# Two attention visits and a routing regrouped in a macaron block of expert FFNs around linear attention

## The chip, the cores and the metric

The kernel runs on one core of a Trainium2 chip. The metric is device time in microseconds (us) of one execution; the kernel before has a median of 237.55 us over three runs (236.08 to 238.13).

## The reference, cut to what matters

The input x is 2 batches of 2048 tokens of width 128, all f32. A routed FFN, a linear attention and the same routed FFN again are added to it, each behind a layer norm.

```python
x = x + 0.5 * ffn(layernorm(x))
x = x + attn(layernorm(x))
x = x + 0.5 * ffn(layernorm(x))

def ffn(x):    # 4 experts, D 128, hidden 512; each token uses the expert of its largest gate logit
    idx = argmax(softmax(x @ Wg + bg))
    return (gelu(x @ W1[idx] + b1[idx]) @ W2[idx] + b2[idx])

def attn(x):   # P = 32 features
    q, k, v = x @ Wq.T, x @ Wk.T, x @ Wv.T
    qp, kp = elu(q @ proj) + 1, elu(k @ proj) + 1
    kv = kp.T @ v                        # 32 x 128, over all tokens of the batch
    return (qp @ kv) / (sum(qp, -1) + 1e-8)
```

## The kernel before, in words

**Phases and visits.** One FFN over one batch is a phase: 0 and 1 are the first FFN over batches 0 and 1, 2 and 3 the second. Before a phase the batch's 16 tiles of 128 tokens are gathered in the order of their experts, by indirect DMAs that GpSimd issues (`gather`, L418). A tile that straddles two experts is computed once for each, with a mask, so a phase has V = 16 + 3 = 19 visits, and the program 76. I write u9 for visit 9 of the phase spoken of. A visit has four `up` products (L966, PSUM banks U), four GELUs on ScalarE (`gelu`, L1145), four `down` products (L977, banks DN) and one VectorE operation that adds the result into the row tile G (`finish`, L729). TensorE works three visits ahead with `up`: after `down` of u(v) comes `up` of u(v+3). Norms (`norm`, L705) and transposes (`turn_in`, L957; copied by ScalarE's `copy_in`, L1139) of the tiles come some visits ahead by the tables NORM_LATE, NORM_MID (phase 1), NORM_EARLY (phase 2) and GROUP_AT. `down` of u(v) waits for `finish` of u(v-2).

**Attention** of batch 0 runs inside phase 1, that of batch 1 inside phase 2, beside the FFN of the other batch. It goes by four groups of four tiles: transposes into bank S1 (`side_turn`, L991), a copy by ScalarE (`side_copy`, L1154), the key, query and gate products (`side_kq`, L998), scaled by VectorE (`la_scaled`, L750 to L752), exp on ScalarE (`la_exp`, L1176), elu and the scaled keys (`la_features`, L758 and L762), the sum over tokens (`la_sum`, L1009), the division (`la_z`, L770 to L773), a fold and the product with Wv (`la_fold`, `la_kv`), the transposed queries (`la_q`, L1021). Then for each group `lb_num` (L1033) makes the result in S1, and `lb_x2` (L793 to L799) adds it to x and takes mean and variance; the next group's `lb_num` waits until the add L793 has read S1. GpSimd raises the variance to -1/2 (`pow_lb`, L406).

**Routing of the second FFN** follows in the same phase, by the number HOT1: `route_hot` at u(HOT1) on VectorE marks each token's expert (hot); `counts` on TensorE counts them; `route_slots` on VectorE (L637 to L651) makes each token's place and the one-hot table A; `place_lanes` and `hots` on ScalarE, `place_tiles` on GpSimd (AV from A) and `route_hots` on VectorE (L656, SL) make the operands of `inverse` (L940, 16 small bf16 products), whose result `route_src` turns into the row indices that `gather` of the next-but-one phase reads. `visit_tables` and `visit_masks` follow later.

**The order** of the work is written out by hand, one list for each engine, indexed by phase and visit; semaphores connect them. GpSimd's list is one queue: the powers, `place_tiles`, and all 64 gathers and 32 scatters. A scatter (`scatter`, L442) writes one finished tile of the second FFN to the output. Ahead of most DMAs stands a memset of a spare tile (L416; 512 or 256 columns), which waits until the previous DMA is issued. In phase 2 GpSimd issues 7 scatters of batch 0 between its other work, then from u(FIRST1) = u11 the 16 gathers of phase 3, and then, outside the visit loop, the 25 remaining scatters.

Of the kernel before, what the change touches and what calls it, by code (L numbers as in the profile page):

```python
# [34 lines left out]
def build(nc, x, wq, wk, wv, proj, w1, b1, w2, b2, wg, bg, out):  # L35
# [31 lines left out]
    with ExitStack() as ctx:  # L67
# [142 lines left out]
        NORM_MID = (-5, -4, -3, -2, -1, 0, 0, 1, 1, 2, 2, 3, 4, 5, 7, 8)  # L210
        NORM_EARLY = (-5, -4, -3, -2, -1, 0, 0, 1, 1, 2, 2, 3, 4, 5, 6, 6)
# [59 lines left out]
        HOT0, HOT1 = 5, 7  # L271
# [89 lines left out]
        def _(eng):  # L361
# [117 lines left out]
            SCATTERS = {5: (1,), 6: (2,), 7: (3,), 8: (4,), 9: (5,), 10: (6,)}  # L479
            DONE0, PAIRS1 = 7, 10  # L480
# [51 lines left out]
        def _(eng):  # L532
# [299 lines left out]
            for s in range(2 * B * V):  # L832
                ph, v = divmod(s, V)
                f, b = divmod(ph, 2)
                finish(s)
# [425 lines left out]
```

How the kernel before makes its waits and increments, by code:

```python
def need(eng, stage, j):  # L17
    if j >= 0:
        eng.wait_ge(stage.sem, j + 1)
# [8 lines left out]
    def did(self, instruction, wait=True):  # L28
        instruction.then_inc(self.sem, 1)
        self.n += 1
        if wait:
            self.eng.wait_ge(self.sem, self.n)
# [257 lines left out]
        @block.sync  # L290
# [12 lines left out]
            def store_x(b, h):  # L303
                for i in range(h * XN[b] // 2, (h + 1) * XN[b] // 2):
                    eng.wait_ge(s_x[b][i], 16)
                eng.dma_start(rows0_v[b][:, h * H:(h + 1) * H, 0:D], X0[b][:, h * H:(h + 1) * H, :]).then_inc(s_rows0[b], 16)
# [22 lines left out]
                ph, v = divmod(s, V)  # L329
                if v % CHUNK == (s == 1):
                    need(eng, rt["visit"], ph)
                    v -= v % CHUNK
                    offs.update({ph * V + v + i: e for i, e in enumerate(loaded(eng, v_slab, ph, v, SW))})
                k = s % NSLAB
                need(eng, ffn["hT"], s - NSLAB)
                need_res(eng, s - NSLAB)
                eng.dma_start(slab[k][:, :], W1[:, bass.ds(offs[s], SW)]).then_inc(s_slab[k], 16)
            eng.wait_ge(s_w["w1"], 16)
            eng.wait_ge(s_w["b2"], 16)
            eng.wait_ge(s_foldd, 4)
# [17 lines left out]
        @block.gpsimd  # L360
# [8 lines left out]
            for b in range(B):  # L369
                eng.memset(MR0[b][:, :, :], 0.0).then_inc(s_const, 1)
            eng.wait_ge(s_const, 7)
            for b in range(B):
# [158 lines left out]
        @block.vector  # L531
# [2 lines left out]
            did = chain.did  # L534
            eng.wait_ge(s_const, 17)
            eng.memset(ones_b[:, :], 1.0).then_inc(s_constd, 1)
```

## Time and profile before

| what | us |
|---|---|
| median of the runs shown | 237.55 |
| the profiled execution's own time | 237.53 |
| its span, first to last instruction | 235.8 |
| TensorE busy | 207.2 (88%) |
| GpSimd busy | 160.2 (68%) |
| VectorE busy | 159.4 (68%) |
| ScalarE busy | 126.9 (54%) |

In the profile PE is TensorE's product and PEld its weight load, DVE is VectorE, ACT ScalarE, POOL GpSimd. "Idle before" is how long an engine stood still ahead of an instruction, with what ended the wait; "issue" means that nothing which the profile shows was waited for. The profiled execution is 1.7 us longer than its span, for what lies around the program. The profile names scatters out_dram<-G L442 and gathers G<-rows,src L430.

### The profile page before, as it was taken

The page shows a single profiled execution, that of the slowest core. Times are in us where ns is not written, and L with a number is a line of the kernel's source. Part 1 is how long each engine was busy: PE and PEld are TensorE (multiplying, and loading weights), DVE is VectorE, ACT ScalarE, POOL GpSimd, SP SyncE. Part 2 cuts the span into 40 slices and gives each one's busy share as a digit, 9 for nine tenths or more (in the row PEclk, how much of TensorE's full clock was granted, in tenths as well). Part 3 has the DMA queues.
Part 4 walks back from the last instruction along what each step waited for, and adds up shares of the span by engine and source line. Part 5 has one row for each costly group of instructions (what it writes and reads, how often), then busy time and mean ns, then how long its engine had stood idle before and what let it go on. Part 6 is the DMA issues. An engine that isn't in the chain of part 4 may idle for free. (4 is left out here: it accounts for less than half of the span.)

```text
span 235.8 us, 6375 instructions
## 1 busy us (share of the span) xinstructions
PE 207.2 (88%) x1786; PEld 195.7 (83%) x1786; DVE 159.4 (68%) x641; ACT 126.9 (54%) x406; POOL 160.2 (68%) x225
## 2 busy tenths in 40 slices
PE   8989996996997999999969998999959899999900
PEld 7879996896997988889969897779959899999900
DVE  3699463579688989698887879788776545553400
ACT  1415055567554586635675676825565567765500
POOL 7221888882728687147138888756878888788775
PEclk9999999998899999999999999999979999999985
DMA  4999259982534462326703852517721976662111
GB/s 103 372 321 254 96 199 351 314 212 83 185 110 167 154 215 69 130 106 237 277 0 116 300 206 83 165 61 281 269 79 42 329 274 222 222 221 103 45 56 45
DMA packets 28454, 41.69 MB, mean 177 GB/s; under 512 B 7795, under 2 KB 14851, under 8 KB 28422
## 3 DMA queue, kind: packets, MB, share of 16 engines
q1 hardware_dynamic: 22368, 34.11, 40.5%
q0 software_dynamic: 3072, 6.82, 11.1%
q10 hardware_dynamic: 2982, 0.36, 1.0%
q8 instruction: 16, 0.26, 0.5%
q14 instruction: 16, 0.13, 0.2%
HBM read 9.41 MB, written 6.82 MB: 69 GB/s over the span
## 5 line engine op out<-in xcount | busy, mean ns | idle before, releaser
L1145 ACT ACTIVATE hT<-U,slab 128x128 f32<-128x128 f32 x304 | 86.7, 370 | 56.4 <-PE U L966 56.3
L966 PE MATMUL U<-hT_in,slab 128*128 (+1 forms) x608 | 82.8, 280 | 1.5 <-ACT hT_in L1139 1.3
L977 PE MATMUL DN<-W,hT 128*128 (+1 forms) x608 | 83.7, 282 | 0.2 <-issue 0.2
L966 PEld LDWEIGHTS U<-hT_in,slab 128*128 128x128 f32 x608 | 74.8, 194 | 2.7 <-issue 2.4
L977 PEld LDWEIGHTS DN<-W,hT 128*128 128x128 f32 x608 | 75.4, 195 | 1.4 <-issue 1.2
L430 POOL DMA_INDIRECT G<-rows,src x64 | 62.5, 977 | 15.2 <-issue 10.2
L729 DVE SCALAR_TENSOR_TENSOR G<-DN,mask,G 128x128 f32 (+1 forms) x76 | 26.4, 348 | 27.3 <-PE DN L977 24.6
L416 POOL MEMSET rest<- 128x512 f32 (+1 forms) x78 | 35.4, 454 | 6.3 <-DVE G L729 0.7
L442 POOL DMA_INDIRECT out_dram<-G x32 | 31.6, 988 | 7.3 <-issue 6.3
L705 DVE TENSOR_SCALAR xn<-G 128x128 f32<-128x128 f32 x64 | 23.7, 389 | 9.3 <-DMA G<-rows,src 9.0
L717 DVE SCALAR_TENSOR_TENSOR G<-slab,mask,G 128x128 f32 (+1 forms) x60 | 21.2, 353 | 6.7 <-DVE G L729 4.0
L1139 ACT ACTIVATE hT_in<-TR 128x128 f32<-128x128 f32 (+1 forms) x44 | 14.4, 327 | 17.8 <-PE TR L957 17.4
L957 PE MATMUL TR<-ident,xn 128*128 128x128 f32 x64 | 14.6, 280 | 7.5 <-DVE xn L705 6.3
L401 POOL TENSOR_TENSOR RS<-VE,neghalf 128x4 f32<-128x4 f32 x8 | 8.5, 1062 | 12.9 <-DVE VE L741 12.8
L406 POOL TENSOR_TENSOR G<-VE,neghalf 128x4 f32<-128x4 f32 x8 | 8.3, 1043 | 12.8 <-DVE VE L799 12.6
L957 PEld LDWEIGHTS TR<-ident,xn 128*128 128x128 f32 x64 | 8.3, 142 | 8.8 <-DVE xn L705 7.2
L898 PE MATMUL DN<-mean_w 128*128 128x128 f32 x104 | 14.6, 300 | 1.1 <-POOL mean_w L362 1.1
L898 PEld LDWEIGHTS DN<-mean_w 128*128 128x128 f32 x104 | 13.9, 215 | 1.1 <-POOL mean_w L362 1.1
L467 POOL TENSOR_TENSOR AV<-A,lane_f 128x256 bf16<-128x256 bf16 x4 | 3.3, 828 | 12.5 <-DVE A L651 6.9
L396 POOL TENSOR_TENSOR MR<-VE,neghalf 128x8 f32<-128x8 f32 x4 | 6.7, 1679 | 5.7 <-DVE VE L564 5.2
L734 DVE BATCH_NORM_STATS2 ST<-G 128x6 f32<-128x128 f32 x32 | 8.8, 287 | 1.6 <-issue 1.4
L656 DVE TENSOR_TENSOR SL<-slot_i,lane_b 128x512 bf16<-128x512 int32 x12 | 8.8, 784 | 0.0
(159 smaller groups left out, 219.7 us busy)
## 6 DMA issues: line engine op xcount, KB each, us to landing
slab<-W SPq DMA_DIRECT2D x76, 322.0 KB, 3.1
rows<-G SPq DMA_DIRECT2D x8, 288.0 KB, 2.1
rows<-X SPq DMA_DIRECT2D x4, 512.0 KB, 9.5
X<-in_L_attn_x_dram SPq DMA_DIRECT2D x4, 256.0 KB, 6.7
X<-in_L_attn_x_dram SPq DMA_DIRECT2D x2, 512.0 KB, 8.8
W<-in_L_ffn_W_dram SPq DMA_DIRECT2D x1, 1024.0 KB, 11.5
W<-in_L_ffn_W_dram SPq DMA_DIRECT2D x4, 256.0 KB, 6.0
G<-rows,src POOLq DMA_INDIRECT x64, 3.2
```

The source lines that it names most:

```text
L416: eng.memset(rest[:, 0:columns], 0.0)
L430: eng.indirect_dma_start(out=row(f, b, t, 0, RW), out_offset=None, in_=(rows0, rows1)[f][b], in_offset=bass.IndirectOffsetOnAxis(ap=src[f] ...
L442: eng.indirect_dma_start(out=out_rows, out_offset=bass.IndirectOffsetOnAxis(ap=index, axis=0), in_=row(1, b, t), in_offset=None, engine_se ...
L705: ffn["norm"].done(eng.tensor_scalar(xn[k % NXN][:, :], row(f, b, t), row(f, b, t, D, 1), row(f, b, t, D + 1, 1), ALU.subtract, ALU.mult))
L717: ffn["res"].done(eng.scalar_tensor_tensor(out=r, in0=slab[s % NSLAB][:, F + NC:SW], scalar=mask[f][b][:, v:v + 1], in1=r, op0=ALU.mult, o ...
L729: ffn["out"].done(eng.scalar_tensor_tensor(out=r, in0=DN[s % 2][:, 0:D], scalar=mask[f][b][:, v:v + 1], in1=r, op0=ALU.mult, op1=ALU.add))
L898: eng.matmul(DN[0][:, 0:P], mean_w[:, :], mean_w[:, :], start=True, stop=True)
L957: last = eng.transpose(TR[:, i * P:(i + 1) * P], xn[k % NXN][:, :], ident[:, :])
L966: i = eng.matmul(U[s % 3][:, c * P:(c + 1) * P], slab[s % NSLAB][:, c * P:(c + 1) * P], hT_in[ph % 2][:, bass.ds(v * P - expert_at[s], P)] ...
L977: i = eng.matmul(DN[s % 2][:, 0:D], hT[s % NHT][:, c * P:(c + 1) * P], W2[:, bass.ds(expert_at[s] + c * NE * D, D)], start=(c == 0 and not ...
L1139: ffn["xTs"].done(eng.activation(hT_in[ph % 2][:, first * P:(first + n) * P], TR[:, 0:n * P], ACT.Copy))
L1145: i = eng.activation(hT[s % NHT][:, c * P:(c + 1) * P], U[s % 3][:, c * P:(c + 1) * P], ACT.Gelu, bias=slab[s % NSLAB][:, F + c:F + c + 1])
```

## The change

- TensorE: `side_turn` of group 3 comes ahead of `down` of u0 and `side_kq` at u0 (was u1). `la_fold` moves from u3 to u2, `la_kv` and `la_q` stand together in u3. The four `lb_num` are at u3, u4, u4, u5 (were u4, u4, u5, u6).
- ScalarE: one run of four exps at u0 behind the copy of group 3 (was three at u18 of the phase before and one at u1), so no copy or wait lies between them; the table loads stay two in each of these phases.
- VectorE: `la_scaled` of group 3 at u0 behind the norms; features in two runs of two groups; one `la_z` over all 16 tiles (was 12 and 4); `lb_x2` at u3, u4, u5, u5 (were u4, u4, u5, u6). The norm tables of phases 1 and 2 leave u1 and u2 free and put two norms each into u3, u4 and u5.
- Routing: HOT1 is 6 instead of 7. `counts` comes at u8, ahead of `up`, instead of u9 behind it; `inverse` at u10 in both phases (was u11 in phase 1, u10 in phase 2). In `route_slots` two small operations (end_i, flo_i) leave for `visit_tables`.
- GpSimd: FIRST1 becomes 10, so phase 3's gathers begin in u10; 6 scatters stand ahead of them instead of 7, and 26 behind them instead of 25.

```diff
-        NORM_MID = (-5, -4, -3, -2, -1, 0, 0, 1, 1, 2, 2, 3, 4, 5, 7, 8)
-        NORM_EARLY = (-5, -4, -3, -2, -1, 0, 0, 1, 1, 2, 2, 3, 4, 5, 6, 6)
+        NORM_MID = (-5, -4, -3, -2, -1, 0, 0, 0, 3, 3, 4, 4, 5, 5, 7, 8)
+        NORM_EARLY = (-5, -4, -3, -2, -1, 0, 0, 0, 3, 3, 4, 4, 5, 5, 6, 6)
...
-        HOT0, HOT1 = 5, 7
+        HOT0, HOT1 = 5, 6
...
-                if ph > 0 and v == 4:
-                    pow_lb(o, 0)
-                if ph == 2 and v == 4:
-                    scatter(0, 0)
-                if ph > 0 and 4 <= v < 3 + NG:
-                    pow_lb(o, v - 3)
+                if ph > 0 and v in (4, 5, 6):
+                    pow_lb(o, v - 4)
+                if ph > 0 and v == 6:
+                    pow_lb(o, 3)
...
-            SCATTERS = {5: (1,), 6: (2,), 7: (3,), 8: (4,), 9: (5,), 10: (6,)}
-            DONE0, PAIRS1 = 7, 10
+            SCATTERS = {v: (v - 4,) for v in range(4, FIRST1)}
+            DONE0, PAIRS1 = FIRST1 - 4, 10
...
-                if v >= FIRST1:
+                if FIRST1 <= v < FIRST1 + T // 2:
...
-                did(eng.tensor_copy(end_i[:, :], c3[:, 0:NE - 1, T - 1]))
-                did(eng.tensor_scalar(flo_i[:, :], end_i[:, :], 7, None, ALU.arith_shift_right))
...
-                    if v == 4:
-                        lb_x2(o, 0)
                         lb_x2(o, 1)
-                    if v in (5, 6):
-                        lb_x2(o, v - 3)
+                    if v == 5:
+                        lb_x2(o, 2)
+                        lb_x2(o, 3)
...
+                if ph in (1, 2) and v == 0:
+                    side_turn(o, NG - 1)
                 down(s)
+                if ph in (1, 2):
+                    if v == 3:
+                        la_kv(o)
+                        la_q(o)
+                    if v == 4:
+                        lb_num(o, 1)
+                    if v == 5:
+                        lb_num(o, 3)
...
-                if ph == 0 and v == hot_at + 2:
+                if ph < B + 1 and v == hot_at + 2:
                     counts(ph + 1)
...
-                    if v == hot_at + 2:
-                        counts(ph + 1)
-                    if v == hot_at + (3 if ph == 2 else 4):
+                        la_fold(o)
+                    if v in (3, 4):
+                        lb_num(o, 2 * (v - 3))
+                    if v == hot_at + 4:
                         inverse(ph + 1, 0, NG)
...
-                if late and v == 1:
-                    la_exp(ph - 1, 3, 4)
...
                         side_copy(o * NG + NG - 1)
+                        la_exp(o, 0, NG)
...
-                if ph < B and v == 18:
-                    la_exp(ph, 0, 3)
```

The first place is TensorE in phase 2, where the counts of the routing stand. U are `up` products, DN `down` products, TR transposes, and S<-hot the counts. Before, end of `down` of u9 and what follows:

```order
L977 ISA
L977 MATMUL DN<-W,hT 128x128
L966 ISA
L966 MATMUL U<-hT_in,slab 128x128 x4
L930 MATMUL S<-hot,ones_b 128x64
L931 MATMUL S<-hot,below_b 128x64
L974 ISA
L974 MATMUL DN<-B2s,ones_b 128x128
```

Now, end of `down` of u8 and what follows:

```order
L977 ISA
L977 MATMUL DN<-W,hT 128x128
L957 MATMUL TR<-ident,xn 128x128 x2
L930 MATMUL S<-hot,ones_b 128x64
L931 MATMUL S<-hot,below_b 128x64
L966 ISA
L966 MATMUL U<-hT_in,slab 128x128 x4
L264 TENSOR_LOAD v_exp_0
```

The counts moved ahead by two `up` and one `down`; `inverse` of this phase stands where it stood.

The second place is VectorE in phase 1, from the writing of KV on: G_1<-DN is a `finish`, G_0<-S with the three rows behind it one `lb_x2`, xn a norm. Before:

```order
L786 TENSOR_TENSOR KV<-S,blocks 128x512
L705 TENSOR_SCALAR xn<-G_1 128x128
L729 ISA
L729 SCALAR_TENSOR_TENSOR G_1<-DN,mask_1,G_1 128x128
L793 TENSOR_TENSOR G_0<-S,G_0 128x4x128
L796 BN_STATS ST_0<-G_0 128x6 x4
L798 BN_AGGR G_0<-ST_0 128x2 x4
L799 TENSOR_SCALAR VE_0<-G_0 128x4
```

Now:

```order
L785 TENSOR_TENSOR KV<-S,blocks 128x512
L728 SCALAR_TENSOR_TENSOR G_1<-DN,mask_1,G_1 128x128
L704 TENSOR_SCALAR xn<-G_1 128x128 x2
L792 TENSOR_TENSOR G_0<-S,G_0 128x4x128
L795 BN_STATS ST_0<-G_0 128x6 x4
L797 BN_AGGR G_0<-ST_0 128x2 x4
L798 TENSOR_SCALAR VE_0<-G_0 128x4
L728 ISA
```

The first `lb_x2` now stands behind the `finish` of u3 and two norms, a `finish` of u4 behind it; before, the first two `lb_x2` stood together behind the `finish` of u4.

The third place is GpSimd behind the loop, where the scatters change from batch 0 (G_0) to batch 1 (G_1). Before:

```order
L416 MEMSET rest 128x256
L442 DMA out_dram<-G_0 4096x128 x2
L416 MEMSET rest 128x256
L442 DMA out_dram<-G_0 4096x128
L442 DMA out_dram<-G_1 4096x128
```

Now:

```order
L416 MEMSET rest 128x256
L442 DMA out_dram<-G_0 4096x128 x2
L416 MEMSET rest 128x256
L442 DMA out_dram<-G_1 4096x128 x2
L416 MEMSET rest 128x256
```

One more scatter of batch 0 stands here, and the last run of scatters with no memset between them is behind the eleventh memset instead of the tenth.

## Rows read from the trace of the kernel before

**Rows 1.** The page: busy time of each engine, and the granted clock in 40 slices.

```profile
PE 207.2 (88%) x1786; PEld 195.7 (83%) x1786; DVE 159.4 (68%) x641; ACT 126.9 (54%) x406; POOL 160.2 (68%) x225
...
PEclk9999999998899999999999999999979999999985
```

**Rows 2.** Groups of POOL's instructions from 176 to 236 us: count, busy, mean, idle before.

```profile
L442 POOL DMA_INDIRECT out_dram<-G x25 | 24.2, 967 | 6.2 <-issue 5.3 <-DVE G L729 0.9
L430 POOL DMA_INDIRECT G<-rows,src x16 | 15.4, 965 | 2.7 <-issue 2.7
L416 POOL MEMSET rest<- 128x256 f32 x26 | 8.1, 312 | 1.6
```

**Rows 3.** Timeline of POOL: start, us, instruction, idle before it and its releaser.

```profile
171.56 0.61 POOL L467 TENSOR_TENSOR AV<-A,lane_f 128x256 bf16<-128x256 bf16 x1 [0.60 <-DVE A L651]
...
176.05 0.31 POOL L416 MEMSET rest<- 128x256 f32 x1
...
233.20 0.95 POOL L442 DMA_INDIRECT out_dram<-G  x1 [0.30 <-issue]
```

**Rows 4.** Timeline of PE in phase 2: down of u7, counts, inverse.

```profile
162.46 1.11 PE L977 MATMUL DN<-W,hT 128*128 x8
...
168.31 0.19 PE L930 MATMUL S<-hot,ones_b 128*128 128x64 bf16 x1
...
172.87 0.25 PE L940 MATMUL S<-AV,SL 128*128 128x32 bf16 x4 [2.22 <-DVE SL L656]
...
173.98 0.40 PE L940 MATMUL S<-AV,SL 128*128 128x32 bf16 x8 [0.34 <-DVE SL L656]
```

**Rows 5.** The chain that ended last: start, us, what.

```profile
174.49 1.90 PE DN L977 x8
176.39 1.23 PE U L966 x8
...
223.57 0.36 DVE G L729
```

**Rows 6.** Timeline of DVE: the slots of the routing in phase 1, then in phase 2.

```profile
114.53 0.29 DVE L637 TENSOR_TENSOR_SCAN cum<-S,zeros 128x64 f32<-128x64 f32 x1 [0.48 <-PE S L931]
...
115.25 0.16 DVE L643 CAST end_i<-cum 128x3 int32<-128x3 f32 x1
...
116.40 0.42 DVE L651 TENSOR_TENSOR A<-tile_i,lane_f 128x256 bf16<-128x256 int32 x1
...
117.00 2.31 DVE L656 TENSOR_TENSOR SL<-slot_i,lane_b 128x512 bf16<-128x512 int32 x3
...
168.56 0.29 DVE L637 TENSOR_TENSOR_SCAN cum<-S,zeros 128x64 f32<-128x64 f32 x1 [0.45 <-PE S L931]
...
169.29 0.57 DVE L643 CAST end_i<-cum 128x3 int32<-128x3 f32 x1
...
171.06 0.42 DVE L651 TENSOR_TENSOR A<-tile_i,lane_f 128x256 bf16<-128x256 int32 x1
```

**Rows 7.** Timeline of PE in phase 1: down of u0, a turned tile, down of u7.

```profile
84.49 1.06 PE L977 MATMUL DN<-W,hT 128*128 x8
...
88.48 0.30 PE L957 MATMUL TR<-ident,xn 128*128 128x128 f32 x1 [0.60 <-ACT hT_in L1139]
...
107.99 1.11 PE L977 MATMUL DN<-W,hT 128*128 x8
```

**Rows 8.** Waits of PE from 80 to 190 us: total, times, longest.

```profile
PE U L966 <- ACT hT_in L1139: 1.3, 1, 1.3
PE S L991 <- DVE KM L752: 1.2, 2, 0.7
```

**Rows 9.** Timeline of ACT in phase 1: three exps, then the copy of group 3.

```profile
87.15 1.03 ACT L1176 ACTIVATE KM<-KM 128x256 f32<-128x256 f32 x3
...
88.24 0.58 ACT L1154 ACTIVATE xTs<-S 128x512 f32<-128x512 f32 x1
```

**Rows 10.** Timeline of DVE in phase 1: the first addition of `lb_x2`.

```profile
99.73 0.69 DVE L793 TENSOR_TENSOR G<-S,G 128x512 f32<-128x512 f32 x1 [0.71 <-PE S L1034]
```

More of the change, by code:

```diff
@@ L641, in route_slots @@
                 need(eng, rt["cb"], ph)
-                did(eng.tensor_tensor(wh3[:, :, :], wh[:, :, :], hot[:, :, :], ALU.mult), False)
-                did(eng.tensor_copy(end_i[:, :], c3[:, 0:NE - 1, T - 1]))
-                did(eng.tensor_reduce(pos[:, :], te(wh3), AX.X, ALU.add), False)
-                did(eng.tensor_scalar(flo_i[:, :], end_i[:, :], 7, None, ALU.arith_shift_right))
+                did(eng.tensor_tensor(wh3[:, :, :], wh[:, :, :], hot[:, :, :], ALU.mult))
+                did(eng.tensor_reduce(pos[:, :], te(wh3), AX.X, ALU.add))
                 did(eng.tensor_copy(pos_i[:, :], pos[:, :]))
@@ L661, in visit_tables @@
                 e_no = exp_no[:, 1:NE, 0]
+                ends = cum[:, :].rearrange("p (e t) -> p e t", e=NE)[:, 0:NE - 1, T - 1]
+                did(eng.tensor_copy(end_i[:, :], ends))
+                did(eng.tensor_scalar(flo_i[:, :], end_i[:, :], 7, None, ALU.arith_shift_right))
                 did(eng.scalar_tensor_tensor(out=vis[:, :], in0=flo_i[:, :], scalar=float(T - 1), in1=e_no, op0=ALU.min,
@@ L880, in _ @@
                     if v == 0:
-                        la_features(o, 0, NG - 1)
-                    if v == 1:
-                        la_z(o, 0, NG - 1)
+                        la_features(o, 0, 2)
+                    if v == 3:
+                        lb_x2(o, 0)
                 if ph < B + 1:
@@ L1018, in la_q @@
             def la_q(b):
-                need(eng, la["z"], 2 * b + 1)
+                need(eng, la["z"], b)
                 for g in range(NG):
@@ L1074, in _ @@
                 ph, v = divmod(s, V)
+                hot_at = HOT0 if ph == 0 else HOT1
+                o = ph - 1
+                if ph in (1, 2) and v == 0:
+                    side_turn(o, NG - 1)
                 down(s)
+                if ph in (1, 2):
+                    if v == 3:
+                        la_kv(o)
+                        la_q(o)
[3 more added lines that the diff above has]
+                        lb_num(o, 3)
                 for ahead in groups_of(ph, v):
                     turn_in(*ahead)
-                hot_at = HOT0 if ph == 0 else HOT1
                 if ph in (1, 2):
-                    o = ph - 1
                     if v == 0:
-                        side_turn(o, NG - 1)
-                    if v == 1:
                         side_kq(o, NG - 1)
-                    if v == 3:
-                        la_q(o)
-                        la_fold(o)
-                    if v in (4, 5, 6):
-                        lb_num(o, (0, 2, 3)[v - 4])
-                if ph == 0 and v == hot_at + 2:
+                    if v == 2:
+                        la_sum(o, 2, 4)
+                if ph < B + 1 and v == hot_at + 2:
                     counts(ph + 1)
@@ L1209, in _ @@
                 late = ph in (1, 2) and v in (0, 1, 2)
-                if late and v == 1:
-                    la_exp(ph - 1, 3, 4)
-                if late and v > 0:
-                    gelu(s + UP_LEAD - 1)
                 if ph in (1, 2):
@@ L1217, in _ @@
                         side_copy(o * NG + NG - 1)
+                        la_exp(o, 0, NG)
                     if v == 2:
                         la_part(o)
+                if late and v > 0:
+                    gelu(s + UP_LEAD - 1)
+                if ph in (1, 2):
                     if v == 3:
```

15 lines of the change are left out of this document (5 added, 10 removed).

## The prediction, made before the changed kernel ran

> **What bounds the kernel now.** I read the page first. TensorE is busy 88% of the span, GpSimd 68% [rows 1], so TensorE looks like the bound. Then I asked which engine is never idle at the end. The groups of GpSimd from 176 us on hold 25 scatters, 16 gathers and 26 memsets, with 24.2 + 15.4 + 8.1 = 47.7 us busy and 10.5 us idle. Nearly all of that idle time is "issue", 0.15 to 0.3 us ahead of each DMA [rows 2]. Three scatters name a `finish` of VectorE, 0.9 us in all, but their gaps are no longer than the others, so they did not really wait. The last scatter starts at 233.20, while the last `finish` started at 223.57 [rows 3, 5]. So the end is set by a queue: GpSimd works without a pause from 176.05 to 234.15, 58.1 us, and TensorE's end has some 9 us of slack behind which it may hide. The chain of waits on the page passes from GpSimd to TensorE at 224, which is only the releaser it inferred for a wait of zero length.
>
> What starts that queue? Ahead of it stands AV at 171.56, behind an idle time of 0.60 that ended with A of VectorE; then two scatters (171.56 to 176.05 is 4.49 us) and the first gather's memset [rows 3]. The row indices for that gather come from `inverse`, which ended near 174.4, so at 176.05 they had been there for over a microsecond: GpSimd itself was late. Thus the quantity that decides is the moment A is ready in phase 2, 171.06 + 0.42 = 171.48 [rows 6]. The end is 64.3 us after it.
>
> I count from T7, the start of `down` of u7 in phase 2, 162.46 [rows 4]. A is ready at T7 + 9.0.
>
> **The routing, from T7 to A.** Between T7 and the counts lie today three `down` (0.95 each), three `up` (0.89) and a pair of transposes (0.22): 5.85 us, 162.46 to 168.31 [rows 4]. The change takes away a `down` and two `up`, so TensorE reaches the counts at T7 + 3.1. VectorE must have written hot by then. It works on `lb_x2` of group 3 in u5 now, a visit earlier; its step from there to hot is some 3 us, and I get T7 + 2.9 for it, a tie with TensorE. The first operation of the slots, cum, starts 0.25 after the counts: T7 + 3.3. From cum to A ready took 116.82 - 114.53 = 2.29 us in phase 1 and 171.48 - 168.56 = 2.92 us in phase 2 [rows 6]. Two operations go out of it, about 0.15 us net, since each was issued beside another. That leaves 2.1 to 2.8; I take 2.5. So A is ready at T7 + 5.8 instead of + 9.0: 3.2 us.
>
> The two moved operations cost some 0.4 us in `visit_tables` at u11, behind everything named here.
>
> Why the two phases differ bears on this term. The conversion into end_i took 0.16 us in phase 1 and 0.57 in phase 2 [rows 6]; in phase 1 GpSimd stood still then, in phase 2 it was issuing scatters. The Trainium skill, GPSIMD Engine Reference, Specifications, says that GpSimd shares its SBUF interfaces with VectorE, so that the two contend in some VectorE operations. By that rule the chain is 2.1 wherever GpSimd rests and 2.8 where it works, and A would shift by no more than 0.4 either way of my value. The rows show the difference, not its cause.
>
> **TensorE's stall at `inverse`.** It waited 2.2 us for SL and, with the two pieces behind it, about 2.8 [rows 4], and then ran at a lower clock: `down` took 1.90 and `up` 1.23 where 0.95 and 0.89 are usual, 1.3 us more [rows 5], in the slice in which the page's granted clock falls to 7 tenths [rows 1]. With the counts 1.5 visits earlier, SL is ready at T7 + 5.8 + 0.3 (a `finish`) + 2.3 (three operations, [rows 6]) = T7 + 8.4, and TensorE comes to `inverse` at T7 + 3.1 + 4.8 = 7.9, so a stall of some 0.6 to 1 us stays and the clock should hold. TensorE is thus 3.2 us or more better off here. By the queue above that is worth nothing in itself; only A counts.
>
> **The price in GpSimd's queue.** Two scatters stand between AV and the first gather, as before. But one more scatter stands behind the gathers, with one more memset. A scatter with its gap takes (24.2 + 6.2) / 25 = 1.22 us, a memset with its gap (8.1 + 1.6) / 26 = 0.37 [rows 2]. So the queue from A on grows by 1.6 us, from 64.3 to 65.9. The removed scatter saves nothing, because it stood ahead of A, where GpSimd now will wait longer for A.
>
> **How T7 moves.** Three pieces.
> First, attention, from `down` of u0 to `down` of u7 in phase 1: 84.49 to 107.99, 23.5 us [rows 7]. Adding up the products alone gives about 21.4, so about 2.1 us are waits, the largest known one 0.60 for the copy of a turned tile behind the exps [rows 7]. Those go, since the copy now follows the GELU. New waits come. TensorE asks for the key and query products only 0.1 us after it has turned the next tile, and must wait for that tile's copy and the copy of group 3 (0.58, [rows 9]): 1.0 us. The product of group 3 stands right behind `down` of u5, but needs the addition of group 2, which VectorE does after the `finish` of u5: 0.35 and 0.69 [rows 10] and two signals, 1.25 us. One more wait of 0.2 is at group 2. The sum is 2.5 for 2.1: I forecast 0.3 us slower, and nothing gained by moving. The four exps end at about 89.5 in the time of before (a first exp 0.42 us, then 0.3 each: [rows 9] has 1.03 for three), and the GELU of u3 follows 3 us later, about 1.2 ahead of its `down`. The `la_z` of all groups ends a visit before `la_q` asks for it. So neither is the last wait.
> Second, `inverse` in phase 1. The wait of 1.3 us for ScalarE's copy [rows 8] goes, because ScalarE's part now comes a visit earlier. Another comes: the norm of tile 15 stands in u8 of VectorE behind the three SL operations (2.31, [rows 6]), and the transposes of u10 ask for it 1.3 us too early. One wait takes the other's place; with the shorter way I put the balance at 0.5 us gained.
> Third, side transposes waited for KM 1.2 us in two places in phase 1 [rows 8]; with the tables a visit earlier VectorE is less behind: 0.4 gained.
> Phase 1 gives 0.6 us in all; phase 2's attention I set equal. T7 comes to 161.9.
>
> **Sum.** A at 161.9 + 5.8 = 167.7, 3.8 us earlier; the queue behind it 1.6 longer; span 235.8 - 3.8 + 1.6 = 233.6, and the execution's own time 237.53 - 2.2 = 235.3. The median of the runs shown, 237.55, is the same number. A measurement tells about 1% from no change here, 2.4 us, so the forecast stands just at that line.
>
> Bounds: the slot chain 2.1 to 2.9 (0.4 either way); T7 from 5 us earlier (all new waits of both phases absent) to 1 us later (the phase 1 balance lost as well); AV 0.6 us as in rows 3, or up to a half more. Together 230 to 237; the ends need everything at once.
>
> **Rivals.**
> - *TensorE sets the end.* The Trainium skill, Perfetto Trace Analysis, Identifying the Most-Contended Engine, has one take the engine of highest occupancy as the bound, here TensorE. As a mechanism: the scatters behind the gathers would wait for `finish`, and the end would follow TensorE's stalls. TensorE gains 2.8 + 1.3 - 0.7 at `inverse` and about 0.8 from phase 1: 4.2, so 233.3. For it speaks the page's 88%; against it the slack of 9 us at the end [rows 3, 5].
> - *The new attention waits are half as long.* 1.25 us less in each phase, T7 earlier by 2.5: 232.8. For it: VectorE and ScalarE are idle a third and a half of the time. Against it: the wait for the addition of group 2 is fixed by the written order.
> - *The gain is eaten.* The slots take 2.9, AV half a microsecond more, T7 does not come earlier: A at 162.8 + 3.3 + 2.9 and AV + 0.5, 2.0 us gained, 1.6 given to the extra scatter: 237.1.
> - *Slower: attention starves TensorE in u4 and u5.* `lb_x2` of groups 1 to 3 with two `finish`, four norms and the statistics fill VectorE without a hole; if it falls a microsecond behind, the product of group 3 waits 2.5 instead of 1.25, and the clock falls as it did behind the 2.2 us wait (1.3 us). That is 2.6 per phase, 5.2 in both: 240.5. It costs more than the gain as soon as the two phases together lose 2.2 us. Against it: in u4 and u5 I find VectorE ready half a microsecond ahead of TensorE.
>
> **How the numbers follow.** Forecast 45%, half of it under 235.2; TensorE as the bound 10%; shorter waits 15%; gain eaten 20%; starved 10%. Faster by over 1%: 0.22 + 0.10 + 0.15 and a little, 0.48. Within 1%: 0.23 + 0.19, 0.42. Slower 0.10. The range runs from the case of shorter waits to the eaten gain, 232.7 to 237.4, which leaves the starved case and a tenth of the rest outside.
>
> **What would show it.** In the changed profile GpSimd should stand idle 1 to 2 us ahead of AV in phase 2, then work without a pause to the end, 65.9 us after A; 26 scatters behind the gathers; `inverse` in phase 2 waiting about 1 us for SL, with no slow product behind it; a wait of about 1.2 us of the product of group 3 (L1033) in u5 of both phases; transposes of phase 1 waiting for the norm of tile 15. The argument is wrong if GpSimd pauses among its last scatters, if the end moves by other than A's shift less 1.6, or if T7 moves by more than 2 us.

## The result, and the profile after

The changed kernel takes 243.41 us (median of 4 runs, 242.84 to 244.72), the kernel before 236.81 beside it (4 runs, 235.76 to 238.13): ratio 1.028, 95% interval 1.021 to 1.036. It is slower by 6.6 us; the forecast was 2.2 us faster, and the time lies outside its range of 232.7 to 237.4. The experiments ran on several chips. On two of them every kernel, before included, takes 11 to 19 us more, nearly all of it in the last phase, so times are compared by ratio to the kernel before that ran beside them, and across chips by distances in the trace. On the others before takes 236.39 to 237.28.

The page of the changed kernel, busy time and granted clock:

```profile
PE 207.3 (86%) x1786; PEld 194.0 (80%) x1786; DVE 157.8 (65%) x633; ACT 127.6 (53%) x406; POOL 160.3 (66%) x225
...
PEclk9999999999999999999999999799999999999955
```

All engines have their work of before to within 2 us ([rows 1]), in a span 6.4 us longer (242.2 against 235.8). The loss is waiting.

First the end, where the forecast looked. Groups of POOL from 181.5 to 242 us, the answer to [rows 2]:

```profile
L442 POOL DMA_INDIRECT out_dram<-G x26 | 25.1, 965 | 6.3 <-issue 5.1 <-DVE G L728 1.2
L430 POOL DMA_INDIRECT G<-rows,src x16 | 15.5, 968 | 2.7 <-issue 2.7
L416 POOL MEMSET rest<- 128x256 f32 x26 | 8.2, 314 | 1.6
```

POOL's timeline, as [rows 3]:

```profile
176.42 0.62 POOL L465 TENSOR_TENSOR AV<-A,lane_f 128x256 bf16<-128x256 bf16 x1 [1.88 <-DVE A L647]
...
239.60 0.96 POOL L442 DMA_INDIRECT out_dram<-G  x1 [0.31 <-issue]
```

GpSimd waits 1.88 us for A, then works without a pause to 240.56. From AV to there it is 64.1 us, against 234.15 - 171.56 = 62.6 before: 1.5 more for the extra scatter, as forecast (1.6). PE and DVE in phase 2, as [rows 4] and [rows 6]; one fence for each engine:

```profile
170.67 1.11 PE L977 MATMUL DN<-W,hT 128*128 x8
...
173.94 0.20 PE L930 MATMUL S<-hot,ones_b 128*128 128x64 bf16 x1
...
179.33 0.56 PE L940 MATMUL S<-AV,SL 128*128 128x32 bf16 x16
```

```profile
174.21 0.29 DVE L635 TENSOR_TENSOR_SCAN cum<-S,zeros 128x64 f32<-128x64 f32 x1
...
175.91 0.42 DVE L647 TENSOR_TENSOR A<-tile_i,lane_f 128x256 bf16<-128x256 int32 x1
```

As in the prediction, T7 is the start of `down` of u7 in phase 2, here 170.67, and A is the moment at which the one-hot table A is ready. The counts stand at T7 + 3.3, the slots take 175.91 + 0.42 - 174.21 = 2.1 us, A is ready at 176.33, T7 + 5.7. `inverse` waits for nothing and the clock holds. So the part that the change was about works as worked out. But T7 is 170.67 where [rows 4] has 162.46.

Where does T7 come from? Waits of all engines, 80 to 190 us: total, times, longest (compare [rows 8]):

```profile
DVE LGX L749 <- POOL RS L401: 6.4, 2, 3.9
...
PE S L1033 <- DVE G L792: 3.0, 4, 1.3
...
PE S L1009 <- DVE KR L761: 2.3, 1, 2.3
...
PE TR L957 <- DVE xn L704: 2.2, 3, 1.0
...
PE S L998 <- ACT xTs L1155: 1.7, 2, 0.9
```

The largest, 6.4 us, names an operation that the prediction never speaks of: VectorE waits for RS, the power (variance to -1/2) that GpSimd computes for the attention groups (`pow_la`, L401). `la_scaled` (L749 to L751) cannot begin without it. Now both sides of that wait. POOL's timeline at the turn from phase 1 to phase 2:

```profile
137.23 1.04 POOL L401 TENSOR_TENSOR RS<-VE,neghalf 128x4 f32<-128x4 f32 x1
...
140.75 0.96 POOL L430 DMA_INDIRECT G<-rows,src  x1 [0.16 <-issue]
...
142.51 0.96 POOL L430 DMA_INDIRECT G<-rows,src  x1 [0.15 <-issue]
...
144.27 0.96 POOL L430 DMA_INDIRECT G<-rows,src  x1 [0.15 <-issue]
...
146.03 0.96 POOL L430 DMA_INDIRECT G<-rows,src  x1 [0.15 <-issue]
147.02 1.04 POOL L401 TENSOR_TENSOR RS<-VE,neghalf 128x4 f32<-128x4 f32 x1
```

DVE there:

```profile
138.38 0.17 DVE L749 COPY LGX<-S 128x16 f32<-128x16 f32 x1 [2.47 <-POOL RS L401]
...
141.95 0.43 DVE L740 TENSOR_SCALAR VE<-MV 128x4 f32<-128x4 f32 x1
...
148.16 0.17 DVE L749 COPY LGX<-S 128x16 f32<-128x16 f32 x1 [3.90 <-POOL RS L401]
```

And PE, which pays:

```profile
140.03 0.33 PE L957 MATMUL TR<-ident,xn 128*128 128x128 f32 x1 [0.96 <-DVE xn L704]
...
150.16 0.99 PE L1009 MATMUL S<-G,KR 128*32 128x128 f32 x16 [2.28 <-DVE KR L761]
...
153.70 1.97 PE L966 MATMUL U<-hT_in,slab 128*128 x8
```

The variance of group 3 is written at 142.4, but its power runs at 147.02: the gathers of GpSimd stand ahead of it in the queue, one every 1.76 us. FIRST1 = 10 starts those of phase 1 a visit earlier too, so 12 gathers instead of 10 lie ahead of that power, and the change asks for `la_scaled` of group 3 a visit sooner (u0 instead of u1). Behind the wait, the sum over tokens waits 2.28 us, and an `up` then takes 1.97 us instead of 1.06, at a granted clock of 0.57 between 152 and 156 us, the 7 in the page's row.

Against [rows 4, 7], counted by the starts of `down`, the loss grows so: 84.51 to 109.02 is 24.5 us for u0 to u7 of phase 1 where before has 23.5 (+1.0); at the first `down` of phase 2 it is +3.4 (141.91 against 138.49); at its u7 +8.2. So the stretch of attention in phase 1 costs 1.0, the rear of phase 1 2.4, the first seven visits of phase 2 4.8. The counting moves a little from one stretch to the next: the four transposes of group 3 (some 0.4 us) now stand ahead of the first `down` of a phase, so they fall to the rear of phase 1 and no longer to the visits behind it.

### The profile page after: what moved, and what is told of

Same layout as the page of the kernel before. It is cut to its first block, busy times and chain, and to the rows that moved or that the text cites. A ratio compares the mean times of both kernels' runs of the same rounds, so it can differ in the third digit from the quotient of the medians.

```text
span 242.2 us, 6366 instructions
## 1 busy us (share of the span) xinstructions
PE 207.3 (86%) x1786; PEld 194.0 (80%) x1786; DVE 157.8 (65%) x633; ACT 127.6 (53%) x406; POOL 160.3 (66%) x225
## 4 chain that ended last, share of the span: by engine, by line
PE 36%; DVE 13%; POOL 8%; issue 6%; DMA 4%; DVEq 1%; ACT 0%; POOLq 0%
PE DN L977 15%; PE U L966 14%; DMA G<-rows,src 3%; POOL out_dram L442 3%; POOL rest L416 3%; DVE G L792 2%; DVE ST L795 2%; PE TR L957 2%; DVE G L728 2%; PE S L1033 2%; POOL G L430 2%; POOL RS L401 1%; PE S L998 1%; PE S L1009 1%; DVE G L797 1%
## 5 line engine op out<-in xcount | busy, mean ns | idle before, releaser
L977 PE MATMUL DN<-W,hT 128*128 (+1 forms) x608 | 81.8, 278 | 1.2 <-DVE G L728 0.8
L977 PEld LDWEIGHTS DN<-W,hT 128*128 128x128 f32 x608 | 73.8, 192 | 2.3 <-issue 2.2
L957 PE MATMUL TR<-ident,xn 128*128 128x128 f32 x64 | 15.2, 289 | 7.5 <-DVE xn L704 7.4
L401 POOL TENSOR_TENSOR RS<-VE,neghalf 128x4 f32<-128x4 f32 x8 | 8.3, 1042 | 11.2 <-DVE VE L740 11.1
L1033 PE MATMUL S<-KV,QT 128*128 128x512 f32 x16 | 8.8, 630 | 3.0 <-DVE G L792 3.0
L998 PE MATMUL S<-Wkq,xTs 128*128 128x96 f32 x64 | 8.5, 275 | 1.7 <-ACT xTs L1155 1.7
```

The costliest lines, as they stand in the source:

```text
L957: last = eng.transpose(TR[:, i * P:(i + 1) * P], xn[k % NXN][:, :], ident[:, :])
L977: i = eng.matmul(DN[s % 2][:, 0:D], hT[s % NHT][:, c * P:(c + 1) * P], W2[:, bass.ds(expert_at[s] + c * NE * D, D)], start=(c == 0 and not ...
```

## The experiments

Theory Q: the powers stand behind more gathers in GpSimd's one queue. Its rival S: the written order of the attention visits is what costs. For a single wait of TensorE in u5 there are W (the wait itself costs time) and V (VectorE is full, and TensorE's waits only mirror it). For the end there are G (the queue from A on sets it) and E (TensorE or `finish` sets it). All kernels below differ from the changed kernel or from before only in what is said of them.

To compare across chips I use two distances in the trace. They came out alike to within 0.1 us wherever the same code ran in that stretch (Z on the chips with the usual last phase only): from the first `finish` of phase 1 to A of phase 2 ready (P), and from AV to GpSimd's last instruction (Z). P + Z moves with the end as long as GpSimd sets it.

| kernel | us | ratio to before, 95% | P | Z |
|---|---|---|---|---|
| before | 236.81 | 1 | 85.9 | 62.6 |
| changed | 243.41 | 1.028 (1.021 to 1.036) | 90.7 | 64.1 |
| e1 gathers of phase 1 from u11 | 238.13 | 1.005 (1.002 to 1.007) | 85.9 | 64.1 |
| e2 routing part alone | 243.08 | 1.023 (1.016 to 1.029) | 90.2 | 64.9 |
| e3 attention part alone | 240.22 | 1.012 (1.005 to 1.019) | 88.2 | 62.8 |
| e4 e2 with gathers from u11 | 240.54 | 1.013 (1.006 to 1.019) | 87.5 | 64.2 |
| e6 e1, product of group 3 behind `up` | 254.23 | 1.018 (1.011 to 1.026) | 85.9 | - |
| e7 e6, norm 15 before the one-hots | 253.35 | - | 86.0 | - |
| e8 changed, shorter memsets in phase 1's gathers | 257.36 | 1.030 (1.023 to 1.037) | 90.3 | - |
| e9 changed, one power earlier | 250.50 | 1.015 (1.005 to 1.026) | 86.5 | - |
| e13 the same kernel, another chip | 238.83 | 1.010 (1.006 to 1.014) | 86.4 | 64.1 |
| e10 e9, a second power earlier | 250.15 | 1.014 (1.001 to 1.027) | 86.9 | - |
| e5, e12 before, shorter memsets | 252.45, 251.16 | 1.011 (1.003 to 1.018), 1.016 (1.004 to 1.027) | 85.9, 85.9 | - |
| e11 e10, shorter memsets | 253.84 | 1.028 (1.016 to 1.040) | 86.9 | - |
| e14 e13, seven scatters ahead | 237.19 | 1.003 (1.000 to 1.007) | 86.4 | 62.6 |
| e15 e14, gathers from u11 | 236.23 | 0.999 (0.996 to 1.002) | 85.1 | 62.6 |
| e16 before, longer memsets | 241.86 | 1.023 (1.014 to 1.032) | 85.9 | 67.9 |
| e18 before, shorter memsets | 233.84 | 0.988 (0.983 to 0.993) | 85.9 | 60.0 |
| e17 e15, shorter memsets | 233.38 | 0.986 (0.980 to 0.991) | 85.0 | 59.9 |

Before was 237.28 beside e1 to e4, 250.32 beside e5 to e8, 247.91 beside e9 to e12, 236.39 beside e13 to e16, 236.63 beside e17 and e18. So e5 to e8 ran on one of the two chips with the longer last phase and e9 to e12 on the other, and their us figures do not compare with the rest. A dash under Z: there Z says nothing, since GpSimd waits for `finish`. e7 has no ratio, because its four times lie too far apart (249.17 to 254.72).

**Which part costs (e1 to e4).** e1:

```diff
+        G1ST = 11
-                if v >= FIRST1:
-                    gather_first(1, 0, s, v - FIRST1)
+                if v >= G1ST:
+                    gather_first(1, 0, s, v - G1ST)
```

(and the same name where phase 1's gathers are counted). e2 is before with HOT1 = 6, the new places of `counts`, `inverse` and end_i and the new scatters, without the attention part; e3 is the changed kernel with those taken back; e4 is e2 with G1ST = 11.

> The changed kernel with one thing put back: phase 2's rows are gathered from u11 of phase 1 again (10 gathers ahead of the last power instead of 12); counts, inverse and attention stay as changed. Theory Q (the powers of the next batch's attention stand behind more gathers in GpSimd's one queue, and VectorE waits for them): the waits of la_scaled for the power, 2.5 and 3.9 us, shrink to under 1.5 each, and with the later start of attention in phase 2 some 4 to 5 us come back: 238 to 239.5. Rival S (the written order of attention and its own waits, 1.3 us at the product of group 3 and 0.9 at the keys, in both phases): the queue hardly matters and the time stays at 242 or above.

> The kernel before with the routing part of the change alone (counts, inverse, slots, first gathers and the scatters as changed; attention and norm tables as before). Theory Q: A of phase 2 stands 5.7 us behind T7 instead of 9.0, the queue behind it is 1.6 us longer, but the power of group 3 comes some 3 to 5 us late and attention of phase 2 waits for it: 237 to 240. Rival S: the loss comes with attention, so this is faster than before, 234.5 to 235.5.

> The changed kernel with the routing part taken back (HOT1 7, counts, inverse, slots, scatters and gathers as before), so attention and norm tables alone. Theory Q: phase 1 loses 1.0 us up to u7 as in the changed kernel's trace and phase 2 about the same plus up to 1 for the power that is now asked for a visit earlier: 2 to 3 us slower than before, 239 to 240. Rival S: the whole loss is here, 242 or above.

> As e2, but with phase 2's rows gathered from u11 of phase 1. Theory Q: the gain of A without the late powers: 236.8 - 3.2 + 1.6 = 235.2, between 234.3 and 236. Rival S: no better than e2.

e1 gives back 5.3 of 6.6 us with one number (P: 4.8), inside what Q expected. DVE in e1 at the place of the 3.90:

```profile
140.63 0.17 DVE L741 TENSOR_SCALAR VE<-MV 128x4 f32<-128x4 f32 x1
...
144.24 0.17 DVE L750 COPY LGX<-S 128x16 f32<-128x16 f32 x1 [1.49 <-POOL RS L402]
```

e3 is 2.9 us above before, within the 2 to 3 expected. Its waits, with those of e2, show how the two moves meet. In before VectorE waits 0.6 us for the power of group 2 and not at all for that of group 3. It waits 2.4 and 1.4 in e2 (12 gathers, asked for in u1), 0.6 and 1.9 in e3 (10 gathers, asked for in u0), and 2.47 and 3.90 in the changed kernel, which does both.

e2 and e4 came out above their ranges, by 3.1 and 4.5 us. The routing alone, even with the gathers back, is slower than before, and the waits of PE in e4 from 150 to 175 us (total, times, longest) say why:

```profile
PE S L932 <- DVE hot L633: 2.1, 1, 2.1
```

In phase 1 of e4 the same wait is 2.23 more. With the routing a visit sooner but the last attention product and its statistics still at u6, VectorE has both in hand and the counts wait for hot; in phases 1 and 2 of the changed kernel no such wait is over 0.3 us. The two halves of the change need each other, which their separate runs could not show as a sum.

**Is VectorE full, and is it the memset? (e6 to e8).** e6 is e1 with the product of group 3 in u5 moved behind `up`, which should cover most of the 1.3 us wait for the addition; e7 also norms tile 15 before the one-hots; e8 shortens the spare memset ahead of phase 1's gathers from 512 to 128 columns:

```diff
-                gather(f, b, 3 * k // 2)
+                gather(f, b, 3 * k // 2, columns=P)
```

> As e1 (changed kernel, gathers of phase 1 from u11), and the product of group 3 in u5 stands behind up of u8 instead of ahead of it. The wait of 1.3 us for the addition of group 2 is then covered by 0.9 us of up. Theory W (this wait is the written order's and TensorE's time counts up to A of phase 2): 0.9 us less per phase, T7 of phase 2 1.8 us earlier, so 236.3 against 238.1 in e1. Rival V (VectorE is what is full in u4 to u7, and TensorE's waits only mirror it): T7 moves, hot does not, the total stays within 0.5 of e1.

> As e6, and in u8 of phase 1 the norm of tile 15 stands ahead of the one-hots of the routing. The wait of the transposes in u10 of phase 1 (0.8 us) goes: 0.5 to 0.8 us below e6 if TensorE's time counts there; no change if VectorE or GpSimd set the pace of phase 1's end.

> The changed kernel as it is (12 gathers ahead of the last power of phase 1, 26 scatters behind the loop), but with memsets of 128 columns instead of 512 ahead of the gathers that phase 1 issues. Each gather takes some 0.3 us less in GpSimd's queue, so the last power comes about 3.5 us earlier. Theory Q: the waits of 2.5 and 3.9 us for the powers fall below 1 and the total falls to 238.5 to 240 without moving a gather. Rival: if it was not the time in the queue but the gathers' transfers or VectorE's own order that made attention late, it stays above 242.

P is 85.9 and 86.0 against 85.9 of e1: nothing gained, the answer of V. (Their times, on a chip with the longer last phase, can't be set against e1's 238.13.) The waits of PE, 80 to 175 us, in e1:

```profile
PE S L1034 <- DVE G L793: 3.0, 4, 1.3
PE TR L958 <- DVE xn L705: 1.4, 2, 0.8
```

and in e7:

```profile
PE S L933 <- DVE hot L631: 1.7, 2, 1.0
PE S L1036 <- DVE G L793: 1.2, 4, 0.4
```

The wait for the addition falls from 3.0 to 1.2 us and that for the norm goes, and a wait for hot of 1.7 us takes their place. In both, `down` of u7 in phase 1 comes 1.0 us sooner than in e1, as soon as in before, and `down` of u12 no sooner than in e1. VectorE's row of results from u3 to u8 is nearly full (in e1 it is busy 9.4 of the 10 us from 100 to 110), and TensorE meets it at one place or another. e8 missed its forecast. The memset takes 0.20 instead of 0.53 us, but GpSimd's queue hardly moves; two gathers of e8:

```profile
139.58 0.20 POOL L416 MEMSET rest<- 128x128 f32 x1
140.24 0.96 POOL L430 DMA_INDIRECT G<-rows,src  x1 [0.46 <-issue]
141.32 0.20 POOL L416 MEMSET rest<- 128x128 f32 x1
141.98 0.96 POOL L430 DMA_INDIRECT G<-rows,src  x1 [0.46 <-issue]
```

One every 1.74 us, against 1.76 in the changed kernel: the idle "issue" ahead of the DMA grew from 0.16 to 0.46. What holds it there I did not find; in phase 3 the same edit does shorten the step (below). So in this stretch only the place of the power in the queue can help.

**The place of the power (e9, e10, e13).** e9 and e13 are one kernel, the changed one with

```diff
-                if ph < B and v == V - 1:
+                if ph == 0 and v == V - 1:
                     pow_la(ph, NG - 1)
...
+                if v == V - 2:
+                    pow_la(1, NG - 1)
                 if v >= FIRST1:
                     gather_first(1, 0, s, v - FIRST1)
```

so that the power of group 3 stands ahead of the last two gathers of u17. e10 also puts that of group 2 between the two gathers of u13.

> The changed kernel, with one line moved: GpSimd raises the variance of attention group 3 of batch 1 ahead of the last two gathers of u17 instead of behind them. The gathers start in u10 as in the change. Theory Q (the power stands behind too many gathers in GpSimd's one queue, and that is why u7 of phase 2 starts late): the statistics were ready near 142.1, so the power starts near 142.5 instead of 147.02, VectorE's wait of 3.9 us for it in phase 2 shrinks to under 1 us, A of phase 2 comes 4 us earlier and the time is 238.5 to 240, about 1.6% under the changed kernel. Rival S (the written order of the attention visits is what costs): the power comes earlier, but A of phase 2 stays within 1 us of 176.3 and the time at 243.

> As the run before, and the power of group 2 between the two gathers of u13 instead of behind those of u13 and u14. Theory Q: it starts near 134.5 instead of 137.23, the wait of 2.5 us of VectorE in u16 goes, and the rear of phase 1 is up to 1.5 us shorter: 237 to 238.5, at or below the version with gathers from u11 (which measured 238.13 against 237.28). Rival: VectorE is what is full there, and the time is within 0.5 us of the run before.

> The changed kernel with the power of attention group 3 of batch 1 ahead of the last two gathers of u17, again, on whatever chip comes. Theory Q: A of phase 2 is 86.5 us after the first finish of phase 1 (90.7 in the changed kernel, 85.9 in before), and where before has 237 the time is 238.5 to 240. Rival S: the time stays at 243 there.

POOL in e13:

```profile
143.45 1.04 POOL L401 TENSOR_TENSOR RS<-VE,neghalf 128x4 f32<-128x4 f32 x1
```

DVE in e13:

```profile
145.06 0.17 DVE L751 COPY LGX<-S 128x16 f32<-128x16 f32 x1 [0.67 <-PE S L1000]
```

The power starts 3.6 us earlier, VectorE's wait for it is gone (what is left, 0.67, is for the key and query product), and P falls from 90.7 to 86.4, the same on two chips; e13 takes 238.83, ratio 1.010. One power, with all gathers where the change put them, gives back 4.3 us of P and 1.8% of the time (ratio 1.010 for 1.028, intervals that do not meet). That is Q. e10 missed: phase 1 ends 1.6 us sooner, but between the two powers GpSimd issues an unbroken row of five gathers, so that the power of group 3 does not come 1.6 us sooner with it, and VectorE waits 1.8 us for it again: P is 0.4 longer than in e9.

**What sets the end (e16, then e14, e15).** e16 is before with `columns=4 * P` for `columns=2 * P` ahead of phase 3's gathers and of the scatters behind the loop: work that nobody reads, put on GpSimd only.

> The kernel before, with memsets of 512 instead of 256 columns ahead of the gathers of phase 3 and of the scatters behind the loop: 0.21 us more each (0.52 for 0.31), 26 of them in one unbroken queue, 5.5 us. Theory G: the time grows by 4.5 to 5.5 us where before has 237 (242), and all of it lies between AV and the end. Rival E (TensorE sets the end): TensorE has some 9 us of slack behind which the queue would hide, so the time grows by under 1 us. Where before has 248 to 250: if its longer last phase comes from gathers issued too closely, the slower pace gives some of it back.

Its groups of POOL, 176 to 242 us:

```profile
L416 POOL MEMSET rest<- 128x512 f32 x25 | 13.1, 526 | 1.5
```

25 memsets of 256 columns took 7.9 us in e14, so these are 5.2 us longer; P stays 85.9, Z grows by 5.3 and the time by 5.5. TensorE's slack of 9 us hides none of it: G, not E. e14 is e13 with one scatter more ahead of A, where GpSimd stood idle 1.90 us; e15 is e14 with the gathers of phase 1 from u11, as in e1:

```diff
-            SCATTERS = {v: (v - 4,) for v in range(4, FIRST1)}
-            DONE0, PAIRS1 = FIRST1 - 4, 10
+            SCATTERS = {4: (0,), 5: (1,), 6: (2,), 7: (3, 4), 8: (5,), 9: (6,)}
+            DONE0, PAIRS1 = 7, 10
```

> As the run before, and seven scatters instead of six ahead of the gathers of phase 3 (two of them in u7, where GpSimd stood idle 1.88 us ahead of AV), 25 behind. Theory G (the queue from A on sets the end): A does not move, the stretch from AV to GpSimd's end falls from 64.1 to 62.6 and the time by 1.6 us: 237 to 238.4 where before has 237. Rival E: the time stays within 0.5 us of the run before, or A moves later by the scatter's 1.2 us.

> As the run before, and the gathers of phase 1 from u11 as in the kernel before. The version with gathers from u11 measured 238.13 against 237.28 and had waits of 1.49 and 0.59 us of VectorE for the powers; the power of group 3 can now start 1.5 us earlier, and the queue is 1.6 us shorter. Theory Q with G: 235 to 236.3 where before has 237.3, the best version. Rival: VectorE is full, the power's 1.5 us are lost again, 236.5 to 237.

POOL in e15, ahead of AV:

```profile
169.16 0.96 POOL L443 DMA_INDIRECT out_dram<-G  x1 [0.16 <-issue]
170.30 0.62 POOL L466 TENSOR_TENSOR AV<-A,lane_f 128x256 bf16<-128x256 bf16 x1 [0.17 <-DVE A L650]
```

DVE in e15, first and last of the slots:

```profile
168.09 0.29 DVE L638 TENSOR_TENSOR_SCAN cum<-S,zeros 128x64 f32<-128x64 f32 x1
...
169.80 0.42 DVE L650 TENSOR_TENSOR A<-tile_i,lane_f 128x256 bf16<-128x256 int32 x1
```

The scatter fits the hole: AV starts 0.08 after A as before, and from e13 to e14 the idle time falls from 1.90 to 0.18, Z from 64.1 to 62.6, the time by 1.64 us (238.83 to 237.19). e15 takes another 1.3 us off P and reaches before, no more: 0.999, a tie. Its 236.23 lies in the range of 235 to 236.3, but that range was written for a before of 237.3, and the gain of 1 to 2.3 us over before that it implied did not come (0.2); the rival, a full VectorE, is nearer.

**A version that beats both (e5, e11, e12, e17, e18).** If GpSimd's queue sets the end, its memsets are the cheapest thing to shorten: `columns=P` there. e5, e12 and e18 are before with that alone, e17 is e15 with it, e11 is e10 with it.

> The kernel before with nothing but shorter memsets ahead of phase 3's gathers and the scatters behind the loop: 128 columns instead of 256, 26 of them. Theory G (GpSimd's queue sets the end from A on): a memset of 512 columns takes 0.52 us and one of 256 takes 0.31, so one of 128 some 0.2; 26 times 0.1 is 2.7 us off the time from AV to the end (62.6 us), and all of it off the total: 234 to 235. Rival E (TensorE, with the highest occupancy, sets the end): no change, 237.

> As the run before, with memsets of 128 instead of 256 columns ahead of the gathers of phase 3 and of the scatters behind the loop. A memset took 0.20 instead of 0.31 us on the other chip and a gather with its memset 1.37 instead of 1.47. Theory G (GpSimd's queue from A on sets the end): 26 memsets are 0.11 shorter, the stretch from AV to the end shrinks from 64.1 to about 61.5, and the time by 2.5 us to 235 to 236. Rival E (TensorE or the landing of gathers sets it): within 0.7 us of the run before, and GpSimd's last scatters wait for finish.

> The kernel before, with memsets of 128 instead of 256 columns ahead of the gathers of phase 3 and of the scatters behind the loop, as in the run on the other chip, whose last phase was some 13 us longer for every kernel and so could not tell. Theory G: AV to the end of GpSimd shrinks from 62.6 to about 60, time 234.5 to 235.3 where before has 237.3. Rival E: within 0.7 us of before. It counts only if before itself is near 237 in this batch.

> The version that measured 236.23 where before has 236.39 (the change with gathers of phase 1 from u11, the power of group 3 ahead of the last gather of u17, seven scatters ahead of the gathers), with memsets of 128 instead of 256 columns ahead of the gathers of phase 3 and the scatters behind the loop: 25 memsets of 0.20 instead of 0.31 us. Theory G: AV to the end 62.6 - 2.7 = 59.9, time 233 to 234 where before has 236.4, 1.1% faster than before. Rival E: the last scatters wait for finish and the time stays within 0.7 us of 236.2. Where before itself is at 248 to 250 it is slower than before, as the two earlier runs were.

> The kernel before with the shorter memsets alone. Theory G: AV to the end 62.6 - 2.7 = 59.9 and the time 233.7 to 234.5 where before has 236.4. Rival E: within 0.7 us of before. Third possibility: the pace of the gathers itself delays other transfers, TensorE stands still in phase 3 and the time is longer than before on this chip too.

e17 takes 233.38 where before has 236.63, ratio 0.986, and e18 233.84, ratio 0.988. Groups of POOL in e17 from 176 us:

```profile
L417 POOL MEMSET rest<- 128x128 f32 x25 | 5.2, 206 | 1.5
```

7.9 - 5.2 = 2.7 us, and the time fell by 2.85 from e15 to e17. Almost all of it is the memset, which the change had not touched; e17 and e18 do not differ by more than their intervals, so nothing here shows that the regrouped order is worth anything beside the memsets. On the two other chips the same edit made before slower: 252.45 against 250.32 (e5) and 251.16 against 247.91 (e12), where 234 to 235.3 was expected, and e11 takes 253.84 where e10 takes 250.15. I would not recommend it without knowing which chip it meets.

## Why the prediction was wrong

**What failed** is one term, T7, forecast 161.9, measured 170.67: 8.8 us. By the prediction's own sign (T7 moves by more than 2 us) its argument is wrong there. Its pieces, by the words of the prediction:

- "phase 2's attention I set equal". It costs 4.8 us. This is the step that turned the sign. I followed the change to FIRST1 only in phase 3, and the sooner `la_scaled` only on VectorE and TensorE, and never asked what stands behind the moved gathers on GpSimd. Both moves meet in the power of group 3. The move of that power alone returns 4.3 of the 4.8 (e13: `down` of u0 to `down` of u7 takes 24.5 us, 28.8 in the changed kernel, 24.0 in before). It was to be read in the trace of before: POOL ran gathers one every 1.8 us there, and the power of group 3 at 142.06, written by 143.24, was asked for at 144.04.
- The rear of phase 1, u7 to the first `down` of phase 2, where the sum had only the two small gains of the last item: +2.4. Of it 1.5 us go with the gathers back at u11 (e1), where the 2.47 us wait for the power of group 2 is 0.6 again; some 0.4 are the transposes of group 3 that now stand there (e3, with the attention part alone, has +0.4). The last 0.5 was not traced.
- Attention of phase 1, forecast +0.3, measured +1.0. The single new waits were right: 0.85 for the copy of group 3 (1.0 forecast), 1.32 for the addition of group 2 (1.25), 0.19 at group 2. What was off is what they replace: I had 2.1 us of waits in the stretch before, worked out as a remainder, but the starts of its neighbouring instructions show some 1.0 (between 86.83 and 88.88, the 0.60 of [rows 7] among them). So the waits are 2.4 for 1.0, and the 0.4 of the transposes that left the stretch make it +1.0.
- `inverse` and the KM waits of phase 1, forecast 0.5 and 0.4 us gained: from u7 to u12 it is 0.1, and the KM waits are 0.90 and 0.26 against 0.69 and 0.54, nothing. Both lie in the rear and its +2.4, so the 0.9 forecast is missing in full. The wait for norm 15 came as forecast (0.77) and took the other's place.

In sum 4.8 + 2.4 + 0.7 + 0.5 + 0.4 = 8.8.

**What held.** GpSimd's queue sets the end: behind A it never pauses, from A to the end of the span are 242.2 - 176.33 = 65.9 us, the number forecast, and lengthening the queue by 5.3 us lengthens the kernel by 5.5 (e16), shortening it by 2.6 shortens it by 2.8 (e18). A comes at T7 + 5.7 (5.8 forecast), partly because two errors cancel: cum starts at T7 + 3.5, not 3.3, and the slots take 2.1, not 2.5. The extra scatter costs 1.5 to 1.6 (e13 to e14). GpSimd waits 1.88 us ahead of AV (1 to 2). The stall at `inverse` and its low clock are gone, even its last microsecond. Where I cited the Trainium skill, GPSIMD Engine Reference, Specifications, on the shared SBUF interfaces: the slots took 2.1 us in phase 2, with GpSimd idle ahead of AV during most of them; by that rule the lower value was to be expected, and it came. But e15, which puts a scatter there, does not bear out what I made of the rule: GpSimd is busy 1.8 us during the slots (0.3 in the changed kernel), and they still take 2.1 (168.09 to 170.22; e14 the same). So a working GpSimd alone did not make this chain 2.8, and why it took 2.9 in before stays open.

**The rivals.** "TensorE sets the end" is refuted by e16, and so is that use of the Trainium skill, Perfetto Trace Analysis, Identifying the Most-Contended Engine: the engine of 88% was not the bound, that of 68% was. (That section of the Trainium skill judges TensorE not by the busy share of its products but by the arithmetic done against the peak and by the busy share of its weight loads. The latter is 83% in [rows 1] and names TensorE too.) The shares of the whole span mislead here: in before from 206 to 236 us GpSimd is busy 22.5 us and TensorE 18.4. The slower rival, starved by attention in u4 and u5, had a sign near the truth but the wrong place: the product of group 3 waits 1.32, not 2.5, and the clock falls at 153.70, in the first visits of phase 2, behind the wait for the power, not there.

**What stays open.** Of P in e13, 86.4 against 85.9 in before, and 85.1 in e15 where VectorE waits 0.6 us for a power: the routing sooner by a visit and a half gains 3.3 us from T7 to A, and the attention's new order loses most of that again. Part of that is VectorE's full row from u3 to u8 (e6, e7), part the wait for the copy of group 3 and the powers; how the rest divides was not settled.

## What to carry to other kernels

When a number moves the start of a stream of DMAs that an engine issues, list everything else in that engine's list behind each place where the number is used, in every phase, and ask who waits for it: a 1 us operation behind two more gathers cost more than the whole gain. A tiny result that another engine waits for belongs ahead of the bulk work in a queue. Where a queue sets the end, test it by adding useless work to it alone: it answers in one run what shares of busy time cannot.

## What the runs showed of the hardware that was not expected

- The step from one indirect DMA to the next on GpSimd was 1.76 us with a memset of 0.53 and 1.74 with one of 0.20 at the turn of phases 1 and 2, while in phase 3 it went from 1.47 (memset 0.31) to 1.37 (0.20). Something other than the memset holds the first step; no run tells what.
- The same program, before with the shorter memsets, took 233.84 us on one chip and 251.16 on another. Up to A they agree (P 85.9 in both). Then, in windows of 10 us of core 0 (PE, PEld, DVE, ACT and POOL busy, clock, DMA share, GB/s), the slower chip:

```profile
180.00:190.00 10.00, 3.75 (x31) 3.56 (x30) 2.39 (x9) 1.14 (x4) 8.52 (x15) 0.88 0.56 184
190.00:200.00 10.00, 3.91 (x19) 3.62 (x19) 0.95 (x3) 1.42 (x5) 8.22 (x15) 0.50 0.30 84
200.00:210.00 10.00, 5.34 (x24) 4.90 (x24) 1.73 (x6) 2.62 (x10) 6.34 (x9) 0.50 0.28 102
```

and the other:

```profile
180.00:190.00 10.00, 9.56 (x84) 9.18 (x83) 6.51 (x26) 6.37 (x23) 8.51 (x15) 1.00 0.74 253
190.00:200.00 10.00, 10.00 (x92) 10.00 (x92) 4.98 (x17) 6.95 (x26) 8.41 (x14) 1.00 0.75 249
200.00:210.00 10.00, 10.00 (x92) 10.00 (x91) 4.82 (x15) 7.17 (x26) 7.90 (x13) 1.00 0.61 220
```

GpSimd issues its gathers at the same pace in both, but on the slower chip VectorE and ScalarE wait up to 9.0 and 7.4 us at a time for something that lies outside the core's engines, the core moves a third of the bytes (84 against 249 GB/s from 190 to 200 us), and TensorE's granted clock is 0.50, its lower level. It begins when phase 3's gathers are issued back to back, and on these chips the kernel with the closer pace was slower than before (1.011, 1.016). That these transfers hold up the slabs on such a chip is a guess; it was not tried.
